# The small transfers of the attention row maxima are issued by ScalarE instead of SyncE

## The chip, the cores and the metric

The kernel runs on one core of a Trainium2 chip. Its time is the device time of one execution in microseconds (us). Engines are named as in the profile: PE is TensorE, ACT is ScalarE, DVE is VectorE, POOL is GpSimd, SP is SyncE. SP computes nothing: it waits on semaphores and issues DMAs.

## The reference, cut to what matters

Two transformer-like blocks (l = 0 and 1 below) work on 1024 tokens of width 256. The part that the change touches is causal softmax attention with 16 heads of width 16, which occurs twice: once in the second block's attention and once in its feed-forward part.

```
q, k, v = heads(...)                       # 16 heads, 16 wide, 1024 tokens
att = einsum('bhqd,bhkd->bhqk', q, k) / 4
att = where(causal, att, -inf)
att = softmax(att)                         # exp(att - rowmax) / sum
y   = einsum('bhqk,bhkd->bhqd', att, v)
```

The rest (layer norms, linear attention, an MLP with packed 4-bit weights, a gated MLP) is left as it is.

## The kernel before

Each engine has its own hand-written list of instructions, in order; semaphores tie the lists together. `wait_ge(S[x], n)` holds an engine's list until semaphore x has reached n, and everything behind it on that engine waits too. A DMA adds 16 to its semaphore when it has landed.

**Attention.** `attention(l)` runs twice, l = 0 and 1. The work is cut into eight blocks (`BLOCKS`, numbered 0 to 7), each of four heads (a group g) and one half c of the queries. Numbered over both attentions, the blocks are n = 0 to 7 and n = 8 to 15. Three bf16 parts of q and k are stacked along the partitions of `qr` and `kr` (96 rows) to give precise scores from bf16 matmuls.

1. For every block PE first computes all scores once, query rows on the partitions ("max" banks, L741, L744 for the causal mask), and DVE reduces each bank to row maxima (L1250). A ring of three PSUM banks lies between them.
2. POOL splits the maxima into three bf16 parts (`m3`), PE transposes them (L750, "rowmax"), ACT copies the result to SBUF (`m3T`, L961, semaphore `m_c`), and four small DMAs, one for each head, bring it into rows 96 to 98 of `qr` (L400, semaphores `m_ld0`, `m_ld1`, 64 counts for a block). They move 3 KB each.
3. PE computes the scores again in the other orientation, now over 99 rows, so that the row maximum is subtracted in the matmul ("score", L764, L767 for the mask). For every key tile there are two such halves of two heads, called score0 and score1 here. The first score of a block waits for that block's `m_ld`.
4. ACT takes the exponential of each half (L952, `pt`, semaphore `ex`), and PE multiplies with v ("value", L778). A value waits for both exponentials of its key tile; a score waits for the exponential two halves earlier, since there are two pairs of PSUM banks for scores.
5. After the last value of a block ACT copies the result out (L968), PE transposes it (L787) and DVE divides it.

The order in which PE, ACT and DVE meet these steps is one list for all three, `ORDER`, which is computed before the kernel runs and which the change leaves alone. In it the max banks of a block come well ahead of its scores from block 2 on: the rowmax of a block stands in the middle of the scores of an earlier block.

**SP's list.** `parts_out` writes the parts of q and k to DRAM (L381, semaphore `pw`), `spread(l, g)` gathers those of group g back into `qr` and `kr` in the stacked layout, twelve DMAs of 128 KB (L391, called the gathers here), and `row_max(l, blk)` waits for ACT's copy and issues the four small DMAs:

```
for l in range(2):
    parts_out(l, 0)
    spread(l, 0)
    spread(l, 1)
    parts_out(l, 1)
    row_max(l, 0)
    spread(l, 2)
    row_max(l, 1)
    spread(l, 3)
    for blk in range(2, len(BLOCKS)):
        row_max(l, blk)
```

All the other loads of the kernel are issued by SP too. ACT issues no DMA.

Of the kernel before, what the change touches and what calls it, by code (L numbers as in the profile page):

```python
# [23 lines left out]
HALF = 512  # L24
# [7 lines left out]
PARTS_ROWS = 96  # L32
# [3 lines left out]
BLOCKS = [(0, 0), (0, 1), (1, 0), (1, 1), (2, 0), (2, 1), (3, 1), (3, 0)]  # L36
# [24 lines left out]
def p2_cols(c, kt):  # L61

    q0 = max(kt * P, c * HALF)
    return q0, (c + 1) * HALF - q0
# [123 lines left out]
def build(nc, a, out):  # L188
# [13 lines left out]
    with ctx:  # L202
        def sb(name, shape, dt=F32):
            return ctx.enter_context(nc.sbuf_tensor(name, shape, dt))

        def sem(name):
            return ctx.enter_context(nc.semaphore(name))

        def overlay(*groups):
# [31 lines left out]


        ((packed, wf_hi, wf_lo, wd, nib, sgn, dbl, r16, gl, it, it_hi, it_lo), (_, v1, g, qT, cum, km), (nat,),
         (qr, kr)) = overlay(
            [("packed", [P, 3 * F0], I32), ("wf_hi", [P, 2, 6 * P], F32R), ("wf_lo", [P, 2, 6 * P], F32R),
# [46 lines left out]
        m3T = sb("m3T", [P, 2, P], BF16)  # L292
# [27 lines left out]
        S = {n: sem(n) for n in names}  # L320
# [5 lines left out]
        def _(sp):  # L326
# [49 lines left out]
            def parts_out(l, dt):  # L376

                for is_k in range(2):
                    w2 = 2 * dt + is_k
                    sp.wait_ge(S["sp_l"], 2 * (4 * l + w2 + 1))  # L380
                    sp.dma_start(scr[w2], part_sets[l][w2][:, :, :]).then_inc(S["pw"], 16)  # L381

            def spread(l, gp):


                dt, four = divmod(gp, 2)
                if four == 0:
                    sp.wait_ge(S["pw"], 16 * (4 * l + 2 * dt + 2))
                for is_k, (dst, order) in enumerate([(qr, (0, 1, 0, 1, 0, 2)), (kr, (1, 1, 2, 2, 0, 1))]):
                    for slot, part in enumerate(order):  # L390
                        sp.dma_start(dst[DH * slot:DH * (slot + 1), 4 * gp:4 * gp + 4, :],  # L391
                                     scr[2 * dt + is_k, 4 * DH * four:4 * DH * (four + 1), part, :].rearrange(
                                         "(h d) t -> d h t", d=DH)).then_inc(S[f"qr_ld{gp}"], 16)

            def row_max(l, blk):
                n = len(BLOCKS) * l + blk
                g, c = BLOCKS[blk]
                sp.wait_ge(S["m_c"], n + 1)
                for j in range(4):
                    sp.dma_start(qr[PARTS_ROWS:PARTS_ROWS + 3, 4 * g + j, c * HALF:(c + 1) * HALF],  # L400
                                 m3T[12 * j:12 * j + 12, n % 2, :]).then_inc(S[f"m_ld{n % 2}"], 16)

            for l in range(2):
                parts_out(l, 0)
                spread(l, 0)
                spread(l, 1)
                parts_out(l, 1)
                row_max(l, 0)
                spread(l, 2)
                row_max(l, 1)  # L410
                spread(l, 3)
                for blk in range(2, len(BLOCKS)):
                    row_max(l, blk)

            sp.wait_ge(S["s2"], 2 * 2 * len(STEPS))
            sp.wait_ge(S["p1_s"], 2 * len(BANKS))
# [449 lines left out]
        def _(act):  # L866
# [66 lines left out]
            def mlp_operand_hi(u):  # L933

                half, dt = divmod(u, 2)
                act.wait_ge(S["h_f"], u + 1)
                act.copy(h_hi[:, dt, half * HALF:(half + 1) * HALF], t2[:, u % 2, :]).then_inc(S["h_hi_s"], 1)

            def attention(l):
                for what, i, *at in ORDER:  # L940
                    if what == "score":
                        blk, gp, c, kt = STEPS[i]
                        n = 2 * (len(STEPS) * l + i) + at[0]
                        w = p2_cols(c, kt)[1]
                        if i == 0 and at[0] == 0:
                            act.wait_ge(S["pw"], 16 * (4 * l + 4))
                        act.wait_ge(S["s2"], n + 1)
                        if n >= 4:
                            act.wait_ge(S["pv"], n - 3)

                        b = 4 + 2 * at[0]
                        act.activation(pt[:, n % 4, :, 0:w], psum[:, b:b + 2, 0:w], ACT.Exp, scale=0.25  # L952
                                       ).then_inc(S["ex"], 1)
                        if l == 1 and at[0] == 1 and i - SPARE in (1, 3, 5, 7):
                            mlp_operand_hi((i - SPARE) // 2)
                    elif what == "rowmax":
                        n = len(BLOCKS) * l + i
                        act.wait_ge(S["m_t"], n + 1)
                        if n >= 2:
                            act.wait_ge(S[f"m_ld{n % 2}"], 64 * (n // 2))  # L960
                        act.copy(m3T[0:48, n % 2, :], bank[at[0]][:, :].bitcast(BF16)[0:48, 0:P]  # L961
                                 ).then_inc(S["m_c"], 1)
                    elif what == "copy":
                        n = 8 * l + i
                        act.wait_ge(S["pv"], 2 * (len(STEPS) * l + STEPS_END[i]))
                        if n >= 2:
                            act.wait_ge(S["ot"], n - 1)
                        act.copy(osb[:, n % 2, :], bank[3][:, :]).then_inc(S["ob"], 1)  # L968
# [60 lines left out]
            v_copy(0)  # L1029
            split(0)  # L1030
            attention(0)
            attention_out(1)
            for i in range(2):
# [22 lines left out]
            split(1)  # L1056
            v_copy(1)
            attention(1)
            attention_out(2)
            mlp_weights_hi(1, 0)  # L1060
# [589 lines left out]
```

## Time and profile before

| | |
|---|---|
| median of 3 runs | 822.97 us (817.56 to 827.11) |
| the profiled execution | 821.39 us, of which the span of the profile is 819.7 us |
| PE busy | 692.5 us, 84% of the span |
| DVE busy | 478.6 us, 58% |
| ACT busy | 335.1 us, 41% |
| L952, the exponentials | 192 instructions, 148.5 us |
| L400, the small DMAs | 64 issues of 3.0 KB |
| first attention | about 349 to 505 us of the span |
| second attention | about 567 to 725 us of the span |

Times in the rows below are microseconds from the start of the span, unless marked ns. Issuing a DMA does not count as busy time. A busy share is a mean over stages with different limits, so it does not say by itself which engine is waited for. The views used are: the list of waits (who waited for whom), the timeline of one engine (start, duration, engine, line, operation, and in brackets the idle time before it and what ended it), and a table by stretch of time.

### The profile page before, as it was taken

The numbers are of one execution on the slowest core, as the hardware profiler recorded it, in microseconds if no ns is written. First come the engines' busy times: TensorE is split into PE (matmuls) and PEld (weight loads), VectorE is DVE, ScalarE is ACT, GpSimd is POOL, SyncE is SP. The second block draws the span as 40 slices with busy tenths as digits, with TensorE's granted clock in tenths as the row PEclk, the third lists the DMA queues.
The fourth block names the chain that finished last, engine by engine and source line by source line (L and its number), as shares of the span: only waits on it lengthen the run. The fifth ranks groups of instructions, "written<-read, shape, count | busy, mean of one in ns | idle before, by whom it ended". The sixth has DMA issues, their size and how long they took to land.

```text
span 819.7 us, 10877 instructions
## 1 busy us (share of the span) xinstructions
PE 692.5 (84%) x4017; PEld 449.4 (55%) x4017; DVE 478.6 (58%) x975; ACT 335.1 (41%) x537; POOL 166.9 (20%) x222
## 2 busy tenths in 40 slices
PE   5949987999999967188999888585889998889996
PEld 4737757777777756134445324463334452248885
DVE  5783366677667368478989201573689883223223
ACT  4121034333333331323565665551235546744332
POOL 1340121545554409200000000000000000002321
PEclk9975576999999979559999999978599999999999
DMA  8920001000000000795300000019950000050001
GB/s 229 236 81 1 0 2 52 0 1 1 1 1 0 1 0 2 165 188 72 41 2 2 2 1 1 1 76 130 175 79 6 2 2 2 1 151 4 1 0 52
DMA packets 35793, 36.19 MB, mean 44 GB/s; under 512 B 16222, under 2 KB 26476, under 8 KB 35740
## 3 DMA queue, kind: packets, MB, share of 16 engines
q1 hardware_dynamic: 35740, 35.49, 20.2%
q8 instruction: 32, 0.52, 0.3%
q14 instruction: 21, 0.17, 0.1%
HBM read 27.94 MB, written 7.34 MB: 43 GB/s over the span
## 4 chain that ended last, share of the span: by engine, by line
PE 39%; issue 24%; DVE 12%; POOL 11%; ACT 5%; DMA 4%; SPq 4%; POOLq 0%; DVEq 0%; ACTq 0%
POOL it_lo L1570 8%; PE psum L778 7%; PE psum L741 7%; PE psum L764 5%; POOL wd L1553 3%; ACT pt L952 3%; DVE m L1250 2%; PE psum L625 2%; DVE qk L1167 2%; PE psum L637 2%; DMA kr<-parts_scratch 2%; PE psum L435 2%; SPq L328 2%; PE psum L481 2%; PE psum L436 2%
## 5 line engine op out<-in xcount | busy, mean ns | idle before, releaser
L952 ACT ACTIVATE pt<-psum 128x1024 f32<-128x1024 f32 (+1 forms) x192 | 148.5, 810 | 107.4 <-PE psum L767 71.4
L1250 DVE TENSOR_REDUCE mx<-psum 128x1 f32<-128x512 f32 (+3 forms) x216 | 132.0, 665 | 26.1 <-PE psum L741 18.9
L741 PE MATMUL psum<-kr,qr 96*128 96x512 bf16 (+3 forms) x384 | 115.8, 357 | 28.3 <-DMA kr<-parts_scratch 24.9
L764 PE MATMUL psum<-qr,kr 99*128 99x512 bf16 (+3 forms) x384 | 100.5, 338 | 6.8 <-DMA qr<-m3T 5.9
L1570 POOL TENSOR_TENSOR it_lo<-it,it_hi 128x512 fp32r<-128x512 f32 x48 | 67.0, 1396 | 183.6 <-ACT it_hi L990 182.4
L778 PE MATMUL psum<-pt,vp 128*32 128x512 f32 (+3 forms) x768 | 83.7, 508 | 19.7 <-ACT pt L952 19.0
L741 PEld LDWEIGHTS psum<-kr,qr 96*128 96x128 bf16 x384 | 37.4, 102 | 92.9 <-issue 35.8
L435 PE MATMUL psum<-h_hi,wf_hi 128*128 128x512 f32 x192 | 78.3, 408 | 3.9 <-issue 3.9
L437 PE MATMUL psum<-h_hi,wf_lo 128*128 128x512 f32 x192 | 75.6, 394 | 0.0
L436 PE MATMUL psum<-h_lo,wf_hi 128*128 128x512 f32 x192 | 75.3, 392 | 0.0
L1596 POOL TENSOR_SCALAR m<-m 128x16 bf16<-128x16 f32 x16 | 4.0, 252 | 328.8 <-DVE m L1250 175.3
L1320 DVE TENSOR_TENSOR it<-psum,gl 128x512 f32<-128x512 f32 x48 | 33.2, 692 | 60.1 <-PE psum L437 47.3
L764 PEld LDWEIGHTS psum<-qr,kr 99*128 99x128 bf16 x384 | 35.7, 99 | 57.9 <-ACT pt L952 26.5
L1250 DVE TENSOR_REDUCE m<-psum 128x1 f32<-128x384 f32 (+3 forms) x88 | 50.7, 635 | 27.6 <-PE psum L744 27.3
L990 ACT CAST it_hi<-it 128x512 fp32r<-128x512 f32 x48 | 29.7, 620 | 75.2 <-DVE it L1320 75.2
L1309 DVE TENSOR_TENSOR wf_lo<-psum,wf_hi 128x512 fp32r<-128x512 f32 (+1 forms) x48 | 24.5, 553 | 47.0 <-ACT wf_hi L976 47.0
L744 PE MATMUL psum<-tri,identb 128*128 128x128 bf16 x256 | 51.9, 231 | 0.0
L767 PE MATMUL psum<-identb,tri 128*128 128x128 bf16 x256 | 51.4, 224 | 0.0
L986 ACT ACTIVATE gl<-psum 128x512 f32<-128x512 f32 x48 | 28.7, 598 | 53.0 <-PE psum L437 34.9
L1527 POOL TENSOR_TENSOR t<-qk,rope_s 128x256 f32<-128x256 f32 x32 | 34.4, 1096 | 56.7 <-DVE qk L1347 23.1
L1265 DVE RECIPROCAL rd<-psum 128x16 f32<-128x16 f32 x16 | 4.1, 254 | 70.5 <-PE psum L787 70.5
L435 PEld LDWEIGHTS psum<-h_hi,wf_hi 128*128 128x128 f32 x192 | 36.5, 190 | 11.4 <-issue 4.5
(193 smaller groups left out, 1236.5 us busy)
## 6 DMA issues: line engine op xcount, KB each, us to landing
parts_scratch<-parts SPq DMA_DIRECT2D x8, 768.0 KB, 7.9
qr<-parts_scratch SPq DMA_DIRECT2D x48, 128.0 KB, 4.6
kr<-parts_scratch SPq DMA_DIRECT2D x48, 128.0 KB, 7.1
wmod<-in_L_wmod SPq DMA_DIRECT2D x1, 1536.0 KB, 6.3
x<-in_L_attn_x SPq DMA_DIRECT2D x2, 512.0 KB, 4.4
wmod<-in_L_wmod SPq DMA_DIRECT2D x1, 1024.0 KB, 5.8
packed<-in_L_ffn_down_W_packed SPq DMA_DIRECT2D x1, 1024.0 KB, 10.0
qr<-m3T SPq DMA_DIRECT2D x64, 3.0 KB
```

The costliest lines, as they stand in the source:

```text
L435: pe.matmul(dst, st_hi, mv_hi, start=first, stop=False)
L436: pe.matmul(dst, st_hi, mv_lo, start=False, stop=False)
L437: return pe.matmul(dst, st_lo, mv_hi, start=False, stop=last)
L741: m = pe.matmul(b, qr[0:PARTS_ROWS, h, qt * P:(qt + 1) * P], kr[0:PARTS_ROWS, h, ch * HALF:ch * HALF + w], start=True, stop=not diag)
L744: m = pe.matmul(b[:, w - P:w], identb[:, :], tri[:, :], start=False, stop=True)
L764: m = pe.matmul(bank[4 + 2 * at[0] + j][:, 0:w], kr[0:PARTS_ROWS + 3, h, kt * P:(kt + 1) * P], qr[0:PARTS_ROWS + 3, h, q0:q0 + w], start=T ...
L767: m = pe.matmul(bank[4 + 2 * at[0] + j][:, 0:P], tri[:, :], identb[:, :], start=False, stop=True)
L778: m = pe.matmul(bank[3][32 * j:32 * j + 32, q0 - c * HALF:q0 - c * HALF + w], vp[:, kt, 4 * gp + j, :], pt[:, (n + j // 2) % 4, j % 2, 0:w ...
L952: act.activation(pt[:, n % 4, :, 0:w], psum[:, b:b + 2, 0:w], ACT.Exp, scale=0.25).then_inc(S["ex"], 1)
L1250: dve.tensor_reduce(dst, bank[at[0]][:, 0:k * w].rearrange("p (k w) -> p k w", k=k), AX, ALU.max).then_inc(S["p1_mx"], 1)
L1527: q = pool.tensor_tensor(v[0][:, :, i, :], v[1][:, :, 1 - i, :], s.unsqueeze(1).to_broadcast([P, 2 * H, DH // 2]), ALU.mult)
L1570: pool.tensor_tensor(it_lo[:, N % 2, :], it[:, N % 2, :], it_hi[:, N % 2, :].bitcast(F32), ALU.subtract).then_inc(S["it_l"], 1)
```

## The change

`row_max` leaves SP's list. Its four DMAs are issued by ACT instead, directly behind ACT's own copy of the maxima, after a wait for that copy's end. The transfers, their semaphores, sizes and number are the same; SP keeps `parts_out`, the gathers, and all loads and stores.

```diff
-            def row_max(l, blk):
-                n = len(BLOCKS) * l + blk
-                g, c = BLOCKS[blk]
-                sp.wait_ge(S["m_c"], n + 1)
-                for j in range(4):
-                    sp.dma_start(qr[PARTS_ROWS:PARTS_ROWS + 3, 4 * g + j, c * HALF:(c + 1) * HALF],
-                                 m3T[12 * j:12 * j + 12, n % 2, :]).then_inc(S[f"m_ld{n % 2}"], 16)
-
             for l in range(2):
                 parts_out(l, 0)
                 spread(l, 0)
                 spread(l, 1)
                 parts_out(l, 1)
-                row_max(l, 0)
                 spread(l, 2)
-                row_max(l, 1)
                 spread(l, 3)
-                for blk in range(2, len(BLOCKS)):
-                    row_max(l, blk)
...
                         act.copy(m3T[0:48, n % 2, :], bank[at[0]][:, :].bitcast(BF16)[0:48, 0:P]
                                  ).then_inc(S["m_c"], 1)
+                        g, c = BLOCKS[i]
+                        act.wait_ge(S["m_c"], n + 1)
+                        for j in range(4):
+                            act.dma_start(qr[PARTS_ROWS:PARTS_ROWS + 3, 4 * g + j, c * HALF:(c + 1) * HALF],
+                                          m3T[12 * j:12 * j + 12, n % 2, :]).then_inc(S[f"m_ld{n % 2}"], 16)
```

On ACT, before, around the copies for blocks 1 to 3 of the first attention. L961 is the copy of the maxima, L952 an exponential; "waits" names the semaphores.

```order
L961 COPY m3T<-psum 48x128 [waits m_t]
L952 ACTIVATE pt<-psum 128x1024 [waits pv,s2] x3
L961 COPY m3T<-psum 48x128 [waits m_ld0,m_t]
L952 ACTIVATE pt<-psum 128x1024 [waits pv,s2] x7
L952 ACTIVATE pt<-psum 128x2x384 [waits pv,s2] x2
L952 ACTIVATE pt<-psum 128x2x256 [waits pv,s2] x2
L961 COPY m3T<-psum 48x128 [waits m_ld1,m_t]
```

On ACT, now, the same stretch (the copy is now L949, the exponential L940, the small DMAs L954):

```order
L949 COPY m3T<-psum 48x128 [waits m_t]
L954 DMA qr<-m3T 3x4x128 [waits m_c]
L954 DMA qr<-m3T 3x4x128 x3
L940 ACTIVATE pt<-psum 128x1024 [waits pv,s2] x3
L949 COPY m3T<-psum 48x128 [waits m_ld0,m_t]
L954 DMA qr<-m3T 3x4x128 [waits m_c]
L954 DMA qr<-m3T 3x4x128 x3
L940 ACTIVATE pt<-psum 128x1024 [waits pv,s2] x7
L940 ACTIVATE pt<-psum 128x2x384 [waits pv,s2] x2
L940 ACTIVATE pt<-psum 128x2x256 [waits pv,s2] x2
L949 COPY m3T<-psum 48x128 [waits m_ld1,m_t]
L954 DMA qr<-m3T 3x4x128 [waits m_c]
```

Four DMA issues now stand between every copy of maxima and the exponential behind it, 16 times in the program.

On SP, before, from the second `parts_out` of the first attention on:

```order
L381 DMA parts_scratch<-parts 128x3072 [waits sp_l] x2
L400 DMA qr<-m3T 3x4x128 [waits m_c]
L400 DMA qr<-m3T 3x4x128 x3
L391 DMA qr<-parts_scratch 16x4x1024 [waits pw]
L391 DMA qr<-parts_scratch 16x4x1024 x5
L391 DMA kr<-parts_scratch 16x4x1024 x6
L400 DMA qr<-m3T 3x4x128 [waits m_c]
L400 DMA qr<-m3T 3x4x128 x3
L391 DMA qr<-parts_scratch 16x4x1024 x6
L391 DMA kr<-parts_scratch 16x4x1024 x6
L400 DMA qr<-m3T 3x4x128 [waits m_c]
```

On SP, now:

```order
L381 DMA parts_scratch<-parts 128x3072 [waits sp_l] x2
L391 DMA qr<-parts_scratch 16x4x1024 [waits pw]
L391 DMA qr<-parts_scratch 16x4x1024 x5
L391 DMA kr<-parts_scratch 16x4x1024 x6
L391 DMA qr<-parts_scratch 16x4x1024 x6
L391 DMA kr<-parts_scratch 16x4x1024 x6
L381 DMA parts_scratch<-parts 128x3072 [waits sp_l] x2
```

The gathers of groups 2 and 3 stand in a row, and nothing of the row maxima is left on SP.

## Rows read from the trace of the kernel before

**Rows 1.** List of waits, whole span, PE: waiter, for whom, us in total, times, longest.

```profile
PE psum L741 <- DMA kr<-parts_scratch: 24.9, 2, 16.9
PEld psum L778 <- ACT pt L952: 43.0, 77, 1.2
PE psum L764 <- DMA qr<-m3T: 5.9, 4, 2.2
```

**Rows 2.** List of waits of SP, both attentions, same columns.

```profile
SPq L400 <- ACT m3T L961: 157.7, 15, 17.5
SPq L391 <- DMA parts_scratch<-parts: 8.9, 3, 3.1
```

**Rows 3.** Timeline of SP, first attention: start, duration of all, line, what, count.

```profile
358.60 3.56 SPq L400 DMA_DIRECT2D qr<-m3T  x4
362.21 2.88 SPq L391 DMA_DIRECT2D qr<-parts_scratch  x6
...
380.54 2.96 SPq L400 DMA_DIRECT2D qr<-m3T  x4
383.54 2.76 SPq L391 DMA_DIRECT2D qr<-parts_scratch  x6
```

**Rows 4.** Timeline of PE: the first score of blocks 0, 1 and 8.

```profile
363.27 0.61 PE L764 MATMUL psum<-qr,kr 99*128 99x512 bf16 x1 [1.56 <-DMA qr<-m3T]
...
384.61 0.60 PE L764 MATMUL psum<-qr,kr 99*128 99x512 bf16 x2 [1.06 <-DMA qr<-m3T]
...
582.93 0.61 PE L764 MATMUL psum<-qr,kr 99*128 99x512 bf16 x1 [2.23 <-DMA qr<-m3T]
```

**Rows 5.** Timeline of ACT: copies of blocks 2, 3, 4, 6, 7, each with the next exponential.

```profile
388.51 0.26 ACT L961 COPY m3T<-psum 48x128 bf16<-48x128 bf16 x1 [0.41 <-PE psum L750]
389.27 1.02 ACT L952 ACTIVATE pt<-psum 128x1024 f32<-128x1024 f32 x1 [0.50 <-PE psum L764]
...
406.55 0.24 ACT L961 COPY m3T<-psum 48x128 bf16<-48x128 bf16 x1
406.70 0.38 ACT L952 ACTIVATE pt<-psum 128x256 f32<-128x256 f32 x1
...
413.51 0.26 ACT L961 COPY m3T<-psum 48x128 bf16<-48x128 bf16 x1 [0.98 <-PE psum L750]
414.06 0.81 ACT L952 ACTIVATE pt<-psum 128x768 f32<-128x768 f32 x1 [0.29 <-PE psum L767]
...
453.05 0.25 ACT L961 COPY m3T<-psum 48x128 bf16<-48x128 bf16 x1
454.73 0.38 ACT L952 ACTIVATE pt<-psum 128x256 f32<-128x256 f32 x1 [1.43 <-PE psum L767]
...
458.96 0.26 ACT L961 COPY m3T<-psum 48x128 bf16<-48x128 bf16 x1 [0.41 <-PE psum L750]
459.49 1.02 ACT L952 ACTIVATE pt<-psum 128x1024 f32<-128x1024 f32 x1 [0.28 <-PE psum L764]
```

**Rows 6.** Timeline of PE: the instruction that waits for each of these five exponentials.

```profile
390.56 0.64 PE L778 MATMUL psum<-pt,vp 128*32 128x512 f32 x4
...
408.50 0.38 PE L764 MATMUL psum<-qr,kr 99*128 99x512 bf16 x1
...
414.95 0.85 PE L778 MATMUL psum<-pt,vp 128*32 128x384 f32 x8
...
455.33 0.43 PE L778 MATMUL psum<-pt,vp 128*32 128x128 f32 x8
...
460.57 0.64 PE L778 MATMUL psum<-pt,vp 128*32 128x512 f32 x4 [0.68 <-ACT pt L952]
```

**Rows 7.** Table by stretch: from:to, length, busy us (count) of each engine, granted clock, DMA share, GB/s.

```profile
core 0: us, PE busy (x) PEld busy (x) DVE busy (x) ACT busy (x) POOL busy (x), PEclk, DMA share, GB/s
...
384.00:396.00 12.00, 11.27 (x65) 3.79 (x66) 10.46 (x18) 7.21 (x9) 0.95 (x4) 1.00 0.95 133
388.00:457.00 69.00, 68.72 (x571) 32.72 (x568) 61.69 (x109) 38.42 (x57) 3.80 (x17) 1.00 0.12 16
...
606.00:610.00 4.00, 4.00 (x16) 1.02 (x14) 2.67 (x4) 3.00 (x3) 0.64 (x3) 0.57 1.08 157
```

## The prediction

> **What bounds the kernel now.** I read the list of waits first, to see who waits for the two kinds of DMA that the change touches [rows 1]. PE waits for the gathers twice, 24.9 us, 16.9 of it at once: these are the first gathers of each attention, which the change does not move. No later gather is waited for. For the row maxima's DMAs PE waits four times, 5.9 us in all. Much longer, 43.0 us in 77 pieces, none over 1.2 us, is what PE's weight loads for the value matmuls wait for ACT's exponentials. So in the attention PE and ACT run nearly in step, although ACT is busy for 41% of the span only.
>
> The waits of SP come next [rows 2]. For 15 of the 16 row maxima SP stood waiting for ACT's copy, so its queue was free when the maxima were ready: the small DMAs are hardly ever late because of the gathers. Of the four times that SP goes from a `parts_out` to the gathers that need it, three waited for that write and not for the small DMAs.
>
> Then the timelines. Before each attention's block 2 nothing else can be done while the maxima travel. From block 2 on, the rowmax stands among the scores of an earlier block, PE is busy for 68.7 of 69 us and DVE for 61.7 (the stretch 388 to 457 in [rows 7]), and it is here that I look at what stands behind each copy on ACT.
>
> **The change, part 1: ACT is held by four issues.** The price of a small DMA issue is measured on SP only: four take 2.96 us, start of the first to end of the last, or 3.56 us in the first block [rows 3], 0.74 or 0.89 us each. No row shows an issue on ACT. The nearest row is the same DMA on SP, so I take 2.96 us, and 3.0 with a few hundredths for the wait on the copy. The bounds are nothing at all, as the low end, and 3.6 us as the high end. ACT's list is in order, so the next exponential cannot start before the copy's end plus 3.0 us. How late PE gets is that delay less the slack that the exponential's consumer has now. A value follows its exponential after 0.06 us when it waits for it (459.49 + 1.02 to 460.57 [rows 5, 6]); I count 0.05 us as the hop and the rest as slack.
>
> - Block 2: the copy ends at 388.77, the next exponential (score1 of key tile 5) is pushed from 389.27 to 391.77, by 2.50 us. Its value starts at 390.56, 0.27 after its end: slack 0.22. PE is 2.28 us late.
> - Block 3: copy end 406.79, exponential 406.70 to 409.79, 3.09 us. Its consumer is score0 of the next block at 408.50, which needs that PSUM pair free, 1.42 after the end: slack 1.37. PE is 1.72 us late.
> - Block 4: 413.77, exponential 414.06 to 416.77, 2.71 us. It ends at 414.87, the value starts at 414.95: slack 0.03, late by 2.68 us.
> - Block 5 repeats block 2's pattern (a copy, then the second half of a full key tile, with the value behind two more banks). Its delay is estimated like block 2's, a tenth less: 2.2 us.
> - Block 6: 453.30, exponential 454.73 to 456.30, 1.57 us, slack 455.33 less 455.11 less 0.05, that is 0.17: late by 1.40 us.
> - Block 7: 459.22, exponential 459.49 to 462.22, 2.73 us, no slack: late by 2.7 us.
>
> That is 13.0 us for an attention [rows 5, 6]. Blocks 10 to 15 run the same order with the same gaps, so it is 26.0 us for twelve holds. The other four holds (blocks 0, 1, 8, 9) cost nothing on ACT: its next exponential there waits for a score that waits for these very DMAs. Block 1's last issue ended at 383.50, and the score started at 384.61 [rows 3, 4].
>
> Is the lost time given back? Between 388 and 457 PE is never idle for long, and DVE has 7.3 us left in 69 [rows 7]. A hold stops PE after at most two more max banks, so DVE runs dry and is late by nearly the same amount. Behind block 7 there are no max banks left and PE waits for ACT in every key tile (the 0.68 us in the last of [rows 6]). So I count nothing back.
>
> **Part 2: the first two row maxima of each attention.** They come off a queue that also carried other traffic. Block 0's four issues took 3.56 us against 2.96 for block 1's [rows 3], 0.6 us more; block 8's score waited 2.23 us against 1.06 for block 1's [rows 4], 1.17 us more. If a queue of its own removes both, 1.8 us come back; if the cause is the DMA engines, none. I take half, 0.9 us.
>
> **Part 3: the gathers of group 3 move forward.** Those of group 2 stay, since they wait for `parts_out` (their first issue, at 362.21, can come 0.05 us after SP is free at 362.16 and by [rows 2] not much earlier). Those of group 3 are now issued right behind them, at about 368 instead of 383.54. Nobody waits for them [rows 1], so nothing is gained. But twelve gathers keep the DMA engines busy for about 0.95 of 12 us, 11.4 us (the stretch 384 to 396 in [rows 7]); 24 in a row run from about 363 to about 386, and block 1's small DMAs, issued from 380.5 to 383.5, now travel among them. Wholly behind them they would land at about 386.5 instead of 384.6, 1.9 us late, 3.8 us for both attentions; with fair turns, nothing. I take half, 1.9 us.
>
> **The sum.** Plus 26.0, less 0.9, plus 1.9: 27.0 us on the profiled execution's own 821.39 us gives 848.4 us, and I say 848. The profiled execution is 1.6 us below the median of 822.97.
>
> **Rivals.** (a) *Issuing is cheap on ACT, and the result is not slower.* With a price of 0.1 us for an issue a hold is 0.4 us, only blocks 4 and 7 are touched, by 0.1 us each, and the 1.8 us of part 2 is larger: about 820 us. The point from which this decides: a hold of 0.3 to 0.7 us costs less than part 2 gives. The total stays under 1% (8.2 us) up to a hold of 1.5 us, 0.38 us an issue: there blocks 2, 4, 5 and 7 lose 0.8, 1.2, 0.7 and 1.2 us, block 3 0.2. Against it: SP's price for this shape is twice that. For it: no row of ACT.
>
> The Trainium skill has a rule for this ("DMA: Bandwidth & Descriptors", section "Issuing engines are not separate DMA queues"): issuing from several engines saves only the sequencer's time for starting a DMA, which is usually small against the DMA. Here the trace does not agree: 0.74 us an issue is not small beside the 1.1 us from the last issue to the score. By that rule the sum would be rival (a)'s. The same page says under "SWDGE vs HWDGE vs iDMA" that a DMA from ACT is made by the same hardware path as one from SP; by that the price is SP's and the sum stands.
>
> (b) *The price is that of a gather.* A gather's issue takes 0.46 us (2.76 for six [rows 3]). A hold is then 1.84 us, the twelve losses come to 12 us, and the time is 834 us.
>
> (c) *The clock falls in the holds.* In 606 to 610 the granted clock was 0.57 for 4 us, right behind block 9's wait, so that 0.43 of 4, 1.7 us, was lost [rows 7]. If each of the twelve new pauses of some 2 us brings such a stretch, 21 us come on top: 869 us; with half of them 859. Against it: block 1's pause of 1.06 us, with PE and its clock as they were then, was followed by a stretch at 1.00 [rows 4, 7], and around every new pause PE is busy all the time.
>
> (d) *The small DMAs starve among the gathers*, beyond part 3's bound, or an issue on ACT costs more than on SP: a hold of 3.6 us adds 0.6 to each of twelve, 7.2 us, 856 us.
>
> **How the numbers follow.** My forecast, 842 to 855 us, gets 0.66; (b), 828 to 842, 0.10; (a), up to 828, 0.10; (c), above 857, 0.07; (d), around 856 to 862, 0.07. A range from 830 to 861 us leaves out (a), a small part of (b) and the larger half of (c), some 0.18. About 1%, 8 us, is what a measurement of this kernel can tell from no change. Slower by more than that: the forecast, (b), (c) and (d), 0.88 after a little of (b) that falls inside. Within 1%: most of (a), 0.10. Faster: 0.02.
>
> **What would show it.** On ACT's timeline, four issues of 0.7 us behind each copy, and the next exponential 3.0 us behind the copy's end, twelve times with a PE pause of 1.4 to 2.7 us at a value or a score, PE waiting for ACT some 26 us longer in all. The distance from the first to the last block's copy (388.5 to 459.0 in the first attention) should grow by the delays of blocks 2 to 6, 10.3 us. SP's gathers should stand in one row of 24 from 362. Block 1's and 9's scores show part 3, block 0's and 8's part 2. The prediction is wrong if the issues on ACT are short, if exponentials start while issues are still running, or if PE catches up between holds because max banks were waiting for DVE.

## The result and the profile after

The changed kernel takes 875.43 us (median, 869.64 to 880.84) against 823.17 us before: 1.064 times as long, with an interval of 1.055 to 1.073. The profiled execution took 869.64 us, with a span of 867.9 us, 48.2 us more than before. The prediction said 848 us and at most 861 us. The direction was right, the size was not. The other three executions took 873.99 to 880.84 us at a mean granted clock of 0.869 to 0.877, where the profiled one, the fastest of the four, had 0.885. So the shares below are those of the fastest execution, and the clock's share is probably larger in the others, which have no trace.

The list of waits of PE and ACT, whole span, of the changed kernel (L766 is the value product, L752 the score, L940 the exponential, L954 the small DMAs; PEld is the load of a matmul's weights):

```profile
PEld psum L766 <- ACT pt L940: 66.2, 76, 4.0
...
PE psum L766 <- ACT pt L940: 41.0, 43, 3.6
ACT pt L940 <- issue: 37.8, 12, 3.2
...
PE psum L729 <- DMA kr<-parts_scratch: 24.9, 2, 17.4
PE psum L752 <- DMA qr<-m3T: 11.7, 4, 4.8
```

The third row is the mechanism of the prediction: twelve exponentials waited for nothing but ACT's own issues, 3.2 us at most, 37.8 us in all. (That the twelve pieces in the table further down also sum to about 37.8 us is chance.) The wait for the exponentials that was 43.0 us long [rows 1] is 66.2, and the second row, 41.0 us, was this before:

```profile
PE psum L778 <- ACT pt L952: 19.0, 36, 0.7
```

The last row was 5.9 us before. By the forecast's bound it could grow by 4 us, and it grew by 5.8.

One of the twelve places, block 4, on the timelines of ACT and of PE:

```profile
424.23 0.26 ACT L949 COPY m3T<-psum 48x128 bf16<-48x128 bf16 x1 [0.98 <-PE psum L738]
424.52 3.01 ACTq L954 DMA_DIRECT2D qr<-m3T  x4
427.63 0.81 ACT L940 ACTIVATE pt<-psum 128x768 f32<-128x768 f32 x1 [3.15 <-issue]
...
428.50 1.01 PE L766 MATMUL psum<-pt,vp 128*32 128x384 f32 x8 [2.76 <-ACT pt L940]
```

All issues of the line, with the shortest, median and longest duration in ns, first and last start:

```profile
L954 ACTq DMA_DIRECT2D qr<-m3T x64: 728/729/1328, 359.8 to 726.8; - x64
```

The exponential starts 3.14 us behind the copy's end (424.49), where the prediction had 3.0, and PE stands still for 2.76 us, where it had 2.68 us of lateness. An issue costs 0.73 us on ACT against 0.70 on SP. So far the forecast held. What it missed shows in the table by stretch, here from one copy of maxima to the next: block 1 to 2, block 4 to 5, block 5 to 6, and, last, block 13 to 14, which is the same piece of program as block 5 to 6, in the second attention.

```profile
core 0: us, PE busy (x) PEld busy (x) DVE busy (x) ACT busy (x) POOL busy (x), PEclk, DMA share, GB/s
381.25:394.78 13.53, 9.35 (x34) 2.61 (x35) 7.24 (x13) 3.33 (x4) 0.95 (x4) 0.75 0.42 57
...
424.23:448.98 24.75, 21.85 (x152) 9.06 (x152) 18.45 (x33) 12.08 (x17) 0.95 (x4) 0.93 0.00 1
448.98:473.15 24.17, 21.92 (x178) 10.92 (x181) 17.36 (x31) 10.03 (x16) 0.95 (x4) 0.86 0.01 1
...
695.34:716.78 21.44, 19.04 (x178) 10.30 (x181) 17.18 (x31) 9.93 (x17) 0.95 (x4) 1.00 0.01 1
```

And the same program before, block 5 to 6:

```profile
433.97:453.05 19.08, 18.96 (x178) 10.29 (x181) 17.18 (x31) 9.92 (x17) 0.94 (x4) 1.00 0.01 2
```

Block 5's piece took 19.08 us before, 21.44 us with the hold at a granted clock of 1.00, and 24.17 us with the same hold at 0.86: 2.4 us are the hold, 2.7 us more the clock. A granted clock of 0.93 or 0.86 over such a stretch means that part of it ran at the lower level, 1.2 GHz instead of 2.4.

How much longer each piece became (us; the granted clock in brackets where it is not 1.00). The last line goes from block 7's copy to its first score:

| from the copy of block | forecast | after, 1st | after, 2nd | two of four, 1st | PE kept busy, 2nd |
|---|---|---|---|---|---|
| 2 | 2.28 | 2.44 | 2.44 | 1.54 | 2.63 (0.97) |
| 3 | 1.72 | 2.01 | 1.98 | 0.51 | 1.95 |
| 4 | 2.68 | 4.29 (0.93) | 4.34 (0.93) | 1.37 | 2.83 |
| 5 | 2.2 | 5.09 (0.86) | 2.36 | 0.86 | 2.63 |
| 6 | 1.40 | 1.55 | 1.54 | 0.08 | 1.94 |
| 7 | 2.7 | 4.83 (0.91) | 4.87 (0.91) | 1.40 | 2.87 |
| all six | 13.0 | 20.2 | 17.5 | 5.8 | 14.9 |

(The last two columns belong to experiments below. The first attention with PE kept busy took 16.5 us, with one low stretch behind block 7.) From block 2's copy to block 7's copy, the first five rows, it is 15.4 and 12.7 us longer, where the prediction named 10.3 as a sign to look for. The 48.2 us of the profiled execution are 37.8 us in these twelve pieces, 8.4 us in the pieces from block 0's, 1's, 8's and 9's copies (of which 5.3 and 5.0 us behind the copies of blocks 1 and 9), and 2.0 us outside.

The gathers, by SP's timeline after, and block 1's first score by PE's:

```profile
364.86 2.94 SPq L391 DMA_DIRECT2D qr<-parts_scratch  x6
367.84 2.95 SPq L391 DMA_DIRECT2D kr<-parts_scratch  x6
370.83 2.77 SPq L391 DMA_DIRECT2D qr<-parts_scratch  x6
373.64 2.77 SPq L391 DMA_DIRECT2D kr<-parts_scratch  x6
...
388.19 0.61 PE L752 MATMUL psum<-qr,kr 99*128 99x512 bf16 x1 [3.65 <-DMA qr<-m3T]
```

They stand in one row, as forecast, and start no earlier. ACT issued block 1's small DMAs from 381.54 to 384.55, and the score started 3.64 us after the last, against 1.1 us before [rows 3, 4]. The DMA view from 381 to 386 (queue, packets, MB, share of the 16 engines' time) names one data queue only:

```profile
q1 hardware_dynamic: 458, 0.75, 109.0%
```

That is SP's. ACT's queue, q10, has no packet in these 5 us, although its first DMA of the block was issued 4.5 us before their end. Its 60 packets run from 386.00 to 386.89, beside the last of the gathers', which ends at 386.78. Before the change block 1's first score followed its last small packet after 0.39 us; here it is 1.3 us, and a third queue fills the gap. It carries instructions, and one packet of it starts in each of these two tenths of a microsecond (after, 386.3 to 386.4; before, 380.9 to 381.0):

```profile
q8 instruction: 1, 0.02, 97.8%
...
q8 instruction: 1, 0.02, 82.0%
```

97.8% of 16 engines for 0.1 us is one engine for 1.56 us: the packet ends at 387.9 and the score starts at 388.19. Before, the same packet started 0.7 us behind block 1's copy and was through 2.4 us ahead of the score. Now it starts 5.1 us behind the copy, as the gathers run out. The program has 32 packets of this queue, 0.52 MB in all, one for about 251 of its 8034 matmuls and weight loads, so they are probably PE's own instructions. In both attentions of the three versions that put the gathers in a row with block 1 on SP or ACT, this packet ended 0.2 to 0.4 us before the score. So the score probably waited last for its instructions, and not for the maxima; no run separates the two.

### The profile page after: what moved, and what is told of

The parts are those of the page before. It is cut to its first block, busy times and chain, and to the rows that moved or that the text cites. A ratio compares the mean times of both kernels' runs of the same rounds, so it can differ in the third digit from the quotient of the medians.

```text
span 867.9 us, 10877 instructions
## 1 busy us (share of the span) xinstructions
PE 709.1 (82%) x4017; PEld 453.4 (52%) x4017; DVE 479.7 (55%) x975; ACT 336.0 (39%) x537; POOL 167.2 (19%) x222
## 4 chain that ended last, share of the span: by engine, by line
PE 36%; issue 23%; DVE 11%; POOL 10%; ACT 6%; ACTq 5%; DMA 5%; SPq 3%; POOLq 0%; DVEq 0%
PE psum L766 7%; POOL it_lo L1563 7%; PE psum L729 6%; PE psum L752 5%; ACTq L954 5%; ACT pt L940 3%; POOL wd L1546 3%; PE psum L613 2%; DVE qk L1160 2%; PE psum L625 2%; DVE m L1243 2%; DMA kr<-parts_scratch 2%; SPq L328 2%; PE psum L423 2%; DMA qr<-m3T 2%
## 5 line engine op out<-in xcount | busy, mean ns | idle before, releaser
L940 ACT ACTIVATE pt<-psum 128x1024 f32<-128x1024 f32 (+1 forms) x192 | 148.7, 810 | 151.8 <-PE psum L755 67.8
L729 PE MATMUL psum<-kr,qr 96*128 96x512 bf16 (+3 forms) x384 | 118.9, 366 | 28.2 <-DMA kr<-parts_scratch 24.9
L766 PE MATMUL psum<-pt,vp 128*32 128x512 f32 (+3 forms) x768 | 89.9, 542 | 41.5 <-ACT pt L940 41.0
L752 PE MATMUL psum<-qr,kr 99*128 99x512 bf16 (+3 forms) x384 | 106.4, 354 | 16.3 <-DMA qr<-m3T 11.7
L729 PEld LDWEIGHTS psum<-kr,qr 96*128 96x128 bf16 x384 | 37.8, 103 | 95.8 <-issue 41.7
L752 PEld LDWEIGHTS psum<-qr,kr 99*128 99x128 bf16 x384 | 37.0, 103 | 72.4 <-ACT pt L940 28.2
L766 PEld LDWEIGHTS psum<-pt,vp 128*32 128x32 f32 x768 | 15.6, 112 | 71.5 <-ACT pt L940 66.2
```

What stands on the lines that cost most here:

```text
L729: m = pe.matmul(b, qr[0:PARTS_ROWS, h, qt * P:(qt + 1) * P], kr[0:PARTS_ROWS, h, ch * HALF:ch * HALF + w], start=True, stop=not diag)
L752: m = pe.matmul(bank[4 + 2 * at[0] + j][:, 0:w], kr[0:PARTS_ROWS + 3, h, kt * P:(kt + 1) * P], qr[0:PARTS_ROWS + 3, h, q0:q0 + w], start=T ...
L766: m = pe.matmul(bank[3][32 * j:32 * j + 32, q0 - c * HALF:q0 - c * HALF + w], vp[:, kt, 4 * gp + j, :], pt[:, (n + j // 2) % 4, j % 2, 0:w ...
```

## The experiments

All times are medians. Each is set against runs of the kernel before that were made beside it, whose median is given. What is said of single places comes from one profiled execution of each version.

**Gathers moved, all on SP** (834.83 against 823.82 us, ratio 1.014, 1.011 to 1.017).

```diff
                 row_max(l, 0)
                 spread(l, 2)
-                row_max(l, 1)
                 spread(l, 3)
-                for blk in range(2, len(BLOCKS)):
+                for blk in range(1, len(BLOCKS)):
                     row_max(l, blk)
```

> All DMAs stay on SP, but the gathers of group 3 are issued straight behind those of group 2, and block 1's four small DMAs behind them. My theory (the change's 52 us are three things: about 26 of holds on ACT, about 10 of half-clock stretches that the holds set off, about 10 from the gathers' new place, where block 1's small DMAs land only behind all gathers and the clock falls in the wait): 8 to 12 us slower than before, about 833, with block 1's first score starting some 4.5 to 5 us behind the copy's last issue instead of 1.1. Rival one (the small DMAs were late in the change because they were on ACT's own queue): no change, 823. Rival two (everything comes from ACT's issues): no change, 823.

Measured: plus 11 us, with ACT issuing nothing. The pieces behind the copies of blocks 2 to 7 and 10 to 15 are what they were before to 0.01 us. All of it comes from the order of the gathers, and not from ACT. The time is what I expected, the distances are not quite: block 1's first score started 2.7 us behind its last issue and block 9's 5.7 us, where I had 4.5 to 5. Against before, the two scores are 1.6 and 4.6 us further from their copies, 6.2 us in all.

**Only blocks 0 and 1 on ACT** (832.65 against 823.82 us, ratio 1.011, 1.006 to 1.015).

```diff
-                row_max(l, 0)
                 spread(l, 2)
-                row_max(l, 1)
                 spread(l, 3)
                 for blk in range(2, len(BLOCKS)):
                     row_max(l, blk)
...
                                  ).then_inc(S["m_c"], 1)
+                        if i < 2:
+                            g, c = BLOCKS[i]
+                            act.wait_ge(S["m_c"], n + 1)
+                            for j in range(4):
+                                act.dma_start(qr[PARTS_ROWS:PARTS_ROWS + 3, 4 * g + j, c * HALF:(c + 1) * HALF],
+                                              m3T[12 * j:12 * j + 12, n % 2, :]).then_inc(S[f"m_ld{n % 2}"], 16)
```

> ACT issues the small DMAs of blocks 0 and 1 of each attention only, where its next exponential waits for them anyway; blocks 2 to 7 stay on SP; the gathers of groups 2 and 3 stand in a row. My theory: 8 to 12 us slower, about 833, all of it between the copies of blocks 1 and 2 and of blocks 9 and 10, like the run that moves the gathers on SP alone. Rival (what costs is ACT issuing at all, 0.8 us an issue on a shared path): nothing here, 823.

Measured: plus 8.8 us, again nothing in the blocks 2 to 7. ACT's own issues cost nothing where its next exponential waits for them anyway. The DMA view of this run from 385 to 387, where the gathers (q1) end; ACT had issued block 1's four (q10, 60 packets) from 379.79 to 382.80:

```profile
DMA  4487491224100000000000000000000000000000
...
q1 hardware_dynamic: 18, 0.02, 7.0%
...
q10 hardware_dynamic: 46, 0.01, 4.8%
```

14 of the 60 packets had moved just before, from 384.64 on, and the other 46 move beside the last 18 of the gathers', all of them two to five us after their issue. By the first line (the busy share in 40 slices) the DMA engines look quiet from 385.6 on, but the score starts only at 387.00. One engine of 16 is too little for a digit of that line: the instruction packet of the result's section is here too, from 385.27 to 386.83.

```profile
q8 instruction: 1, 0.02, 4.9%
```

4.9% of 16 engines for 2 us is one engine for 1.57 us.

**Block 1 issued by POOL** (840.03 against 825.0 us, ratio 1.016, 1.012 to 1.021). The gathers stand in a row, block 1's DMAs get a semaphore of their own:

```diff
+                    if blk == 1:
+                        pool.wait_ge(S["m_c"], n + 1)
+                        for j in range(4):
+                            pool.dma_start(qr[PARTS_ROWS:PARTS_ROWS + 3, 4 * g + j, c * HALF:(c + 1) * HALF],
+                                           m3T[12 * j:12 * j + 12, n % 2, :]).then_inc(S["m_ldp"], 16)
```

> All on SP with the gathers of groups 2 and 3 in a row, but block 1's four small DMAs are issued by POOL, whose descriptors are made in another way. It tells where the small DMAs wait behind the gathers. If they wait in what SP and ACT share when they issue (my guess, as in the changed kernel ACT's packets moved only after the last gather packet although they had a queue of their own): POOL's packets run among the gathers' and block 1's first score starts 1 to 3 us after the last issue has been made, block 1 no later than with its own queue. Rival (any queue waits until the 16 DMA engines have drained the gathers): the first score starts as late as in the run that moves the gathers on SP, with the packets behind the gathers' last.

Measured: my guess was wrong. POOL issued from 383.05 to 385.41; in the DMA view from 383 to 386.4 there is again SP's queue alone (312 packets) and nothing of POOL's, and the score came 7.7 us behind the copy (10.8 in the second attention) against 4.36 before. POOL's first packet started at 386.64, when the gathers had 0.5 us to go. Three issuing engines, three queues, and the small DMAs waited until the gathers were nearly through each time, and so did the instruction packet, which no engine's list issues. So it is hardly what SP and ACT share when they issue. (How long POOL's DMAs take to start on quiet engines, no run shows.) Why the DMA engines did not take turns earlier stays open.

**Blocks 2 to 7 on ACT only** (868.12 against 823.82 us, ratio 1.056, 1.050 to 1.063). Blocks 0 and 1 stay on SP between the gathers.

```diff
                 row_max(l, 1)
                 spread(l, 3)
-                for blk in range(2, len(BLOCKS)):
-                    row_max(l, blk)
...
+                        if i >= 2:
+                            g, c = BLOCKS[i]
+                            act.wait_ge(S["m_c"], n + 1)
+                            for j in range(4):
+                                act.dma_start(qr[PARTS_ROWS:PARTS_ROWS + 3, 4 * g + j, c * HALF:(c + 1) * HALF],
+                                              m3T[12 * j:12 * j + 12, n % 2, :]).then_inc(S[f"m_ld{n % 2}"], 16)
```

> ACT issues the small DMAs of blocks 2 to 7 only; blocks 0 and 1 stay on SP between the gathers, in their old places. My theory: holds of 3.1 us on twelve places and the clock stretches they set off, 33 to 40 us slower than before, about 860. Rival (the holds alone, as the prediction summed them, and the clock fell only because of the gathers' wait ahead): 26 us slower, 849, with the clock at full all through the blocks 2 to 7.

Measured: plus 44 us, and not the 33 to 40 that I expected; the rival's 26 us at full clock is out. With the 8.8 us of the blocks 0 and 1 on ACT it makes 53 us, and the whole change cost 52. The two parts add up.

**The changed kernel with the gathers held back** (870.34 against 823.82 us, ratio 1.057, 1.052 to 1.062).

```diff
                 spread(l, 2)
+                sp.wait_ge(S["m_ld1"], 256 * l + 64)
                 spread(l, 3)
```

> The changed kernel, but SP waits until block 1's small DMAs have landed before it issues the gathers of group 3. My theory: 10 us faster than the changed kernel, about 862 to 866, with block 1's first score 1.1 us behind the last issue. Rival (an own queue with fair turns costs nothing, and the late landing in the changed kernel came from something else): same as the changed kernel, 875.

Measured: 46.5 us slower than before, against 52 for the change, so 5 to 6 us came back and not 10. Block 1's and 9's scores are at their old distance from the copy (4.42 and 4.43 us against 4.36), but in the profiled execution PE's clock was low in the pieces behind these copies all the same, 0.70 and 0.69 against 1.00 and 0.82 before. What came back is what the two scores had been late, 2.6 and 3.7 us in the changed kernel, 6.3 us together. The low clock behind them did not come from the lateness. The intervals of this run and of the change overlap, so the 5 to 6 us rest on the traces more than on the times.

**Two of the four on ACT** (blocks 2 to 7; 839.49 against 825.0 us, ratio 1.017, 1.013 to 1.021) and **three of the four** (850.54 against 823.52 us, 1.031, 1.023 to 1.038). SP issues the others.

```diff
-                for j in range(4):
+                for j in range(0 if blk < 2 else 2, 4):
                     sp.dma_start(qr[PARTS_ROWS:PARTS_ROWS + 3, 4 * g + j, c * HALF:(c + 1) * HALF],
...
+                        if i >= 2:
+                            g, c = BLOCKS[i]
+                            act.wait_ge(S["m_c"], n + 1)
+                            for j in range(2):
+                                act.dma_start(qr[PARTS_ROWS:PARTS_ROWS + 3, 4 * g + j, c * HALF:(c + 1) * HALF],
+                                              m3T[12 * j:12 * j + 12, n % 2, :]).then_inc(S[f"m_ld{n % 2}"], 16)
```

With three of the four both 2s of the two `range` lines are 3s.

> For blocks 2 to 7 ACT issues two of the four small DMAs and SP the other two; blocks 0 and 1 are as before. My theory (a hold costs the path what the prediction's slack sum says, and the clock falls where the pause of PE grows long): a hold of 1.55 us, twelve times, 8 to 9 us by the slack sum, and few or no half-clock stretches behind the blocks 2 to 7, so 831 to 833, less than a quarter of the 44 us that four issues cost. Rival (the cost goes with the number of issues on ACT): half of 44, 845.

> Like the run with two of four, but ACT issues three of the four for blocks 2 to 7 and SP one: a hold of 2.3 us. By the slack sum alone: 18 us slower, 842. My theory (slack sum plus half-clock stretches that begin with the longer pauses of PE): more than that, 19 to 27 us, with half-clock stretches behind some of the blocks 4, 5 and 7. Rival (the cost goes with the number of issues): three quarters of 44, 33 us, 857.

Measured: 14.5 and 27 us. Two, three and four issues cost 14.5, 27 and 44 us, that is 7.2, 9 and 11 us for each issue of a block: the cost grows faster than the number, as a slack that is used up and then a clock that falls would have it, and neither rival's proportion fits. The three runs alone do not prove that form; the traces carry it. With two, I had a hold of 1.55 us and 8 to 9 us in all, which was too low. The next exponential came 1.65 us behind the copy's end, by which the slack sum is 4.9 us an attention. The first attention lost 5.8 us at full clock (the table above), 0.6 of it because the first two issues that ACT makes in the program took 2.11 us and later pairs 1.52. The second lost 6.5 us, with one low stretch. The whole stretch from block 2's copy to block 7's first score, which took 105.06 us before:

```profile
389.07:499.89 110.82, 97.33 (x783) 42.01 (x783) 63.17 (x112) 63.26 (x87) 4.73 (x20) 1.00 0.08 10
```

With three issues there were low stretches behind blocks 7, 12 and 15, and the 27 us are at the upper end of what I expected.

**Issues spread out** (823.06 us in ten runs against 825.0 us, ratio 0.998, 0.994 to 1.002). ACT issues the same 48 DMAs, one behind each first-half exponential (`issue_one` takes the next from the list, waits for its copy and issues it):

```diff
+                        if i >= 2:
+                            for j in range(4):
+                                pending.append((n, i, j))
...
                                        ).then_inc(S["ex"], 1)
+                        if at[0] == 0:
+                            issue_one()
```

> ACT issues all small DMAs of blocks 2 to 7, the same 48 issues, but not in a row: one behind the first-half exponential of each following key tile. Blocks 0 and 1 as before. My theory (what costs is not an issue on ACT but four of them ahead of an exponential that PE waits for): an issue now lies in the 1.2 us that ACT is idle in a key tile, or delays the next exponential by under 0.8 us; 0 to 8 us slower than before, 823 to 831, no half-clock stretches. Rival (the issues take ACT's time wherever they stand): 26 us or more slower, 849 or more.

Measured: no difference from before. ACT's timeline behind block 2's copy, and the stretch from there to block 7's first score:

```profile
392.62 0.26 ACT L971 COPY m3T<-psum 48x128 bf16<-48x128 bf16 x1 [1.48 <-PE psum L748]
393.38 1.02 ACT L960 ACTIVATE pt<-psum 128x1024 f32<-128x1024 f32 x1 [0.50 <-PE psum L762]
394.25 1.35 ACTq L944 DMA_DIRECT2D qr<-m3T  x1
394.30 1.02 ACT L960 ACTIVATE pt<-psum 128x1024 f32<-128x1024 f32 x1
...
397.39 0.73 ACTq L944 DMA_DIRECT2D qr<-m3T  x1
397.66 1.02 ACT L960 ACTIVATE pt<-psum 128x1024 f32<-128x1024 f32 x1
...
392.62:497.68 105.06, 96.90 (x784) 42.01 (x784) 63.02 (x112) 63.27 (x87) 4.73 (x20) 1.00 0.06 8
```

The issue that stands behind the exponential of 394.30 in the program starts at 394.25, while that exponential begins: ACT's sequencer hands an exponential over and goes on to the next instruction, so the issue hides under it. 105.06 us is what the stretch took before.

**PE kept busy in the holds** (857.54 against 823.52 us, ratio 1.039, 1.032 to 1.047; the run with blocks 2 to 7 on ACT had 1.056, 1.050 to 1.063). That kernel, with nine matmuls whose weights are a tile of zeros, `zz`, added to the value accumulator at the twelve places where PE waits:

```diff
+                def keep_busy():
+                    for _ in range(9):
+                        pe.matmul(bank[3][:, :], zz[0:PARTS_ROWS, :], qr[0:PARTS_ROWS, 0, 0:HALF],
+                                  start=False, stop=False)
...
+                        if (i, at[0]) == (12, 0):
+                            keep_busy()
...
+                        if i in (5, 13, 20, 27, 29):
+                            keep_busy()
                         pe.wait_ge(S["ex"], n + 2)
```

> The run in which ACT issues the small DMAs of blocks 2 to 7, with nine matmuls of zeros (about 2 us at full clock) added on PE at each of the twelve places where it waits out a hold; they add nothing to the sums of the value product. My theory (the part of the 44 us beyond the slack sum is half-clock stretches that PE's pauses bring on): none of the twelve intervals has such a stretch, and in spite of 108 more matmuls it is faster than that run, 26 to 30 us slower than before, 850 to 854. Rival (the surplus is a longer hold or lost overlap, and the clock only goes along with it): no faster than that run, 868 or more.

Measured: with 108 matmuls more it is faster, 34 us slower than before instead of 44. From block 2's copy to block 7's first score, both attentions, first without the zeros:

```profile
394.39:519.37 124.98, 103.29 (x784) 43.05 (x784) 63.59 (x112) 63.38 (x87) 4.76 (x20) 0.95 0.05 7
633.29:761.50 128.21, 106.59 (x784) 44.42 (x784) 71.05 (x123) 65.14 (x90) 4.76 (x20) 0.92 0.06 9
```

and with them:

```profile
391.25:512.85 121.60, 110.58 (x837) 47.19 (x837) 63.26 (x112) 63.35 (x87) 4.76 (x20) 0.99 0.05 7
630.90:750.80 119.90, 109.38 (x837) 47.16 (x837) 70.45 (x123) 64.90 (x90) 4.76 (x20) 0.99 0.04 6
```

PE's clock went from 0.95 and 0.92 to 0.99, and the two stretches are 253.2 and 241.5 us long: 11.7 us less. The holds are as long as they were (ACT waited 39.0 us for its own issues in either run), so the clock is a cause of its own and hangs on PE's pauses. It did not vanish altogether (one low stretch behind block 7), and the zeros probably cost something: block 6's piece grew by 1.94 us with them and by 1.55 without, both at full clock. So it is 34 us and not the 26 to 30 expected.

**Blocks 0 and 1 split between ACT and SP** (820.79 us in seven runs against 825.0 us, ratio 0.9925, 0.989 to 0.996). Each issues two of the four; all other small DMAs and the gathers' order are as before.

```diff
-                for j in range(4):
+                for j in range(2 if blk < 2 else 0, 4):
                     sp.dma_start(qr[PARTS_ROWS:PARTS_ROWS + 3, 4 * g + j, c * HALF:(c + 1) * HALF],
...
+                        if i < 2:
+                            g, c = BLOCKS[i]
+                            act.wait_ge(S["m_c"], n + 1)
+                            for j in range(2):
+                                act.dma_start(qr[PARTS_ROWS:PARTS_ROWS + 3, 4 * g + j, c * HALF:(c + 1) * HALF],
+                                              m3T[12 * j:12 * j + 12, n % 2, :]).then_inc(S[f"m_ld{n % 2}"], 16)
```

> For blocks 0 and 1 of each attention ACT, which is idle there, issues two of the four small DMAs and SP the other two, at the same time; all else as before. My theory: the two engines issue side by side, the first score starts 1.5 us earlier at four places, so 5 to 6 us faster, 817 to 818. Rival (issues of SP and ACT go through one shared path, one after the other): no change, 823.

Measured: 4 to 6 us faster than before, the only version here that beats it. ACT's and SP's issues for block 1, and its first score:

```profile
381.36 1.50 ACTq L967 DMA_DIRECT2D qr<-m3T  x2
...
381.35 1.50 SPq L400 DMA_DIRECT2D qr<-m3T  x2
...
384.21 0.38 PE L764 MATMUL psum<-qr,kr 99*128 99x512 bf16 x1
```

The two run side by side at full speed. From the copy's start to the score it is 3.1 us instead of 4.4. Block 9 gained as much (3.23 instead of 4.36). Blocks 0 and 8 did not measurably. Block 0's distance is 5.23 us against 4.95, block 8's 4.56 against 5.62, and in the six traces where SP issues these small DMAs between the gathers as before, they lie between 4.95 and 6.01 and between 4.33 and 5.62. So two places gained 1.2 and 1.1 us, where I expected 1.5 us at four. Where the rest of the 4 to 6 us comes from is not shown: in the profiled execution PE's clock stayed up behind block 9, but so it did in two of the traces with the old issues.

## Why the prediction was right or wrong

- **The price of an issue** (part 1, 0.74 us from SP's rows): right, 0.75 us (3.01 for four), and rival (a), cheap issues, is out. The Trainium skill calls the time to start a DMA usually small beside the DMA itself ("DMA: Bandwidth & Descriptors", "Issuing engines are not separate DMA queues"). No trace here agrees: an issue takes 0.73 us on ACT, and before the change block 1's first score came 1.1 us behind the last of its issues. In the spread version it costs nothing because it hides under an exponential, not because it is short.
- **The slack sum** (13.0 us an attention): right for the holds. The pieces at full clock grew by 2.44, 2.0, 2.36 and 1.55 us against 2.28, 1.72, 2.2 and 1.40; with the 2.83 and 2.87 us that blocks 4 and 7 cost when PE was kept busy (the zeros' own cost is in them, so they are upper bounds) it makes 14.1 us an attention, 28 for both, where I had 26. Nothing was given back between holds, as forecast.
- **The clock** (rival c): here the prediction failed most. The sum has the clock at nothing. Rival (c) priced a low stretch at 1.7 us, and they cost 1.5 us behind block 4 (4.29 less 2.83) and 2.7 behind block 5, but it got a chance of 0.07, because block 1's pause of 1.06 us had left the clock up and PE is busy around every new pause. Both reasons fail. Longer pauses (2.25 and 2.76 us at blocks 5 and 4) were followed by low stretches in five of twelve places in the changed kernel and eight in the run with the holds alone, against one of twelve with two issues and none in the kernel before. And the row on block 1 was the luck of one execution: of the seven traces in which block 1's first score is 4.36 to 4.42 us behind its copy, five have a low stretch at that score. In the spread version the piece behind block 1's copy, 8.26 us long before at a clock of 1.00, is this:

```profile
381.68:392.62 10.94, 9.33 (x34) 2.58 (x35) 7.23 (x13) 3.33 (x5) 0.94 (x4) 0.69 0.66 90
```

In the twelve pieces of the changed kernel the clock accounts for 37.8 less 28, about 10 us, which is what rival (c) had for half of them.
- **The gathers** (part 3): the sign was right, the bound failed. I took 1.9 us and allowed 3.8 in all; moving the gathers costs 8.8 to 11 us. The small DMAs did wait for nearly the last gather, which was my worst case, but the scores of blocks 1 and 9 came 2.6 and 3.7 us late, where I had 1.9 at most for each. About 0.9 us of either is the time from the last small packet to the score, 1.3 us instead of 0.4, into which the late instruction packet falls: a wait that the sum did not have. Behind block 1's score the clock was low too (0.75 in the piece of 13.53 us), but it was as low with the score in its old place (0.70 with the gathers held back, 0.69 in the spread version), so the lateness is not shown to be its cause. With the order of before, block 1's maxima went first and the gathers followed; that order is worth 1%. The Trainium skill has the DMA engines take turns between queues, packet by packet ("DMA: Bandwidth & Descriptors", "Queues, rings and completion order"). No trace here agrees: in each run with the gathers in a row the small packets started only in the last 0.1 to 1.1 us of the gathers, on ACT's queue up to 5.5 us after the block's first issue.
- **A queue of their own** (part 2, 0.9 us back): not seen. Block 0's and 8's scores started 5.07 and 4.99 us behind their copies, against 4.95 and 5.62, and the run with all on SP had 4.96 and 4.87.
- **The sum again.** On the profiled execution it was 21 us short: 2 us of holds, 10 us of clock, 7 us in the pieces of the first two blocks (8.4 us where the sum had 1.0), 2 us elsewhere.
- **The range** was too narrow since it treated the clock as a separate small chance. A longer pause of PE costs its length and, in 5 to 8 of twelve places here, the clock as well.

## What to carry to other kernels

An issue of a DMA is an instruction that holds its engine's list: look at what stands behind it. Behind an instruction that is still computing it was free here, ahead of one that another engine waits for it cost its length less that engine's slack. When TensorE is made to pause in a tuned program, count the clock on top of the pause: here it was a third again of the holds' price. And before small urgent transfers are freed from a queue, see what moves forward into the place they held.

## What was not expected of the hardware

- Small DMAs waited for the end of a row of gathers on SP's queue, on ACT's and on POOL's. So did a packet of instructions: it started 4.1 to 5.8 us behind block 1's copy instead of 0.6 to 0.8, and ended just before the first score.
- Issues of SP and ACT at the same time do not slow each other: 1.50 us for two on each.
- An issue on ACT runs while ACT computes the exponential ahead of it.
- The first four issues on ACT took 3.62 us (the first of them 1.33), later ones 3.01.
